# Query stage of a gated cross-attention and expert-attention kernel: VectorE works ahead on the groups of x, transposes are spread between projections, loads are reordered, ScalarE scales the last fifteen tiles

## The chip, the cores and the metric

One core of one Trainium2 chip runs the whole program. The metric is the device time of one execution in microseconds (us), lower is better. The program's engines are TensorE (PE; its weight loads PEld), VectorE (DVE), ScalarE (ACT), GpSimd (POOL) and SyncE (SP, which here only issues transfers). They run their own instruction streams in order and meet at semaphores.

## The reference, cut to what matters

x is 32 batches x 100 tokens x 256, all float32; the context is 32 x 361 x 256.

```
x = x + tanh(g_xattn) * xattn(layernorm(x), ctx)      # 16 heads of 16; q from layernorm(x), k and v from ctx
x = x + tanh(g_ffn) * ffn(layernorm(x))               # 8 heads of 128, attention over 100 tokens,
                                                      # values and outputs through 2 of 8 experts per head
# inside xattn
Q = layernorm(x) @ Wq.T + bq;  K = ctx @ Wk.T + bk;  V = ctx @ Wv.T + bv
O = softmax(mask(Q K^T / 4)) V @ Wo.T + bo
```

## The kernel before

The first half of the program (`stage_attention_in`) runs two parts on every engine, one behind the other in program order: the query stage (`stage_queries`) and the cross-attention (`stage_cross`), with the cross-attention's first steps, `start(0)` to `start(6)`, interleaved into the query stage through `between`. The experts' part follows behind a barrier and isn't touched.

**Query stage.** The 3200 tokens of x are 25 tiles of 128 tokens in `big`, in five groups of five, each group one load (640 KB). Per group, VectorE takes mean and variance of each tile (L246, L249), forms 1/std in small steps with one square root on ScalarE (L136 to L146 and `root`, L277), and scales the five tiles in place (L253). TensorE turns each tile with two transposes into `pt`, which has two banks (L306); ScalarE copies it to `xnt` (L284). Then come the projections: 16 units of 4 matmul records each (128 x 400, L316) into the four banks of `pq`. For each unit ScalarE writes a float16 high part (`hi`, L295) and VectorE the rest (`low`, L259). Groups 0 to 4 own units 0-1, 2-5, 6-7, 8-11 and 12-15. TensorE's unit n waits for `low(n - 4)`.

What orders the work is written out by hand. TensorE: five turns, then the units of the group, `between(n - 4)` behind unit n. VectorE: statistics and scaling of group g + 1, then `low` for the units of group g. ScalarE: five copies, the next group's root, then `hi` for the units.

**First steps of the cross-attention.** `start(0)`: TensorE makes the keys of batch 0 (12 matmuls, L727), ScalarE and VectorE their high and low parts (L653, L548). `start(1)`, `start(2)`: values of batch 0 (12 and 6 matmuls, L744; copies L661). `start(3)`: keys of batch 1. `start(4)`: VectorE spreads a bias (L538, L542). `start(5)`: TensorE's output bias (L821, L822). `start(6)`: VectorE scales it by the tanh of the gate (L610), which ScalarE makes behind the last copies (L291). The keys wait until GpSimd has split weights and two contexts into float16 high and low parts (L224 to L238), and GpSimd waits for all weights and biases (`s_cw`, 96).

**SyncE.** It issues, in order: x0, x1, wq, bq, x2, x3, x4, the gates, wk, wv, wo, three biases, two contexts. Then, per quarter of the queries, `between(g)`, the store of the high part and that of the low part (L208, L211). Behind the last quarter it waits until all four quarters have landed (L470), and only then issues batch 1's eight query loads (L414), its mask and x (L419, L421), and the context of batch 3 (L403), which GpSimd splits (L484, L486) and TensorE turns into keys in batch 1's first steps.

The cross-attention itself takes 16 heads per batch, TensorE's first matmul of each is the score (L755); one reciprocal of the denominators (L574) comes once per batch.

Of the kernel before, what the change touches and what calls it, by code (L numbers as in the profile page):

```python
# [29 lines left out]
P = 128  # L30
# [119 lines left out]
def stage_queries(nc, k, sems, cross, big, x, g_xattn, g_ffn, wq_t, bq, ctx_t, weights, biases, q_parts):  # L150


    with ExitStack() as ctx:
# [7 lines left out]
        std, rstd, half = (m.sbuf(n, [P, NT]) for n in ("q_std", "q_rstd", "q_half"))  # L161
        qhi = m.sbuf("q_hi", [P, DC, T], F16)
# [6 lines left out]
        s_cw, s_cx = held.sem("q_s_cw"), held.sems("q_s_cx", 2)  # L169
        s_zero, s_chi, s_clo = (held.sem(f"q_s_{n}") for n in ("zero", "chi", "clo"))  # L170
        s_g, s_tanh = held.sem("q_s_g"), held.sem("q_s_tanh")
# [5 lines left out]
        SHIFT = 4  # L177
# [6 lines left out]

        def sync(sp, between):
            for i in range(GROUPS):
# [3 lines left out]
                if i == 1:  # L190
                    sp.dma_start(wq[:, :, :], wq_t.rearrange("(c p) e -> p c e", p=P)).then_inc(s_w, 16)
                    sp.dma_start(bqc[:, :], bq).then_inc(s_w, 16)
            for i, g in enumerate((g_xattn, g_ffn)):
                sp.dma_start(k.tanh_g[:, i:i + 1], g.partition_broadcast(P)).then_inc(s_g, 16)
            for i, w in enumerate(weights):
                sp.dma_start(cross.w[:, i, :, :], w.rearrange("(c p) e -> p c e", p=P)).then_inc(s_cw, 16)
            bk, bv, bo = biases
            sp.dma_start(cross.bkc[:, :], bk).then_inc(s_cw, 16)
            sp.dma_start(cross.bvc[:, :], bv).then_inc(s_cw, 16)
            sp.dma_start(cross.bor[:, :], bo.rearrange("(a n) -> a n", a=1)).then_inc(s_cw, 16)  # L200
            for b in range(2):
                sp.dma_start(cross.ctxb[:, b, :, :], ctx_t[b, :, :].rearrange("(c p) s -> p c s", p=P)
                             ).then_inc(s_cx[b], 16)
# [10 lines left out]
        def gpsimd(pool):  # L214
# [8 lines left out]
            pool.wait_ge(s_cw, 96)  # L223
# [17 lines left out]
        def vector(dve, between):  # L241
            def normalize_group(g):
                cut = slice(TILES * g, TILES * (g + 1))
                dve.wait_ge(s_x[g], 16)
                for t in tiles(g):
                    dve.bn_stats(st[:, t, :], xt[:, t, :]).then_inc(s_st, 1)  # L246
                dve.wait_ge(s_st, TILES * (g + 1))
                for t in tiles(g):
                    dve.bn_aggr(mv[:, t, :], st[:, t, :]).then_inc(s_mv, 1)  # L249
                dve.wait_ge(s_mv, TILES * (g + 1))  # L250
                rstd_steps(dve, mv[:, cut, :], std[:, cut], rstd[:, cut], half[:, cut], s_step, s_std, 6 * g)
                for t in tiles(g):
                    dve.tensor_scalar(xt[:, t, :], xt[:, t, :], mv[:, t, 0:1], rstd[:, t:t + 1],  # L253
                                      ALU.subtract, ALU.mult).then_inc(s_xn, 1)
# [10 lines left out]
            normalize_group(0)  # L265
            dve.wait_ge(s_w, 32)
            for g in range(GROUPS):
                if g < GROUPS - 1:
                    normalize_group(g + 1)
                for n in units(g):  # L270
                    low(n)

        def scalar(act, between):
# [4 lines left out]

            root(0)
            act.wait_ge(s_w, 32)  # L280
            for g in range(GROUPS):
                for t in tiles(g):
                    act.wait_ge(s_t, t + 1)
                    act.activation(xnt[:, :, t * P:(t + 1) * P],  # L284
                                   pt[:, t % 2, 0:DC * P].rearrange("p (c n) -> p c n", c=DC),
                                   ACT.Copy).then_inc(s_xnt, 1)
                if g < GROUPS - 1:
                    root(g + 1)
                else:
                    act.wait_ge(s_g, 32)  # L290
                    act.activation(k.tanh_g[:, :], k.tanh_g[:, :], ACT.Tanh).then_inc(s_tanh, 1)  # L291
                for n in units(g):
# [4 lines left out]
                    between(n - SHIFT)  # L297

        def tensor(pe, between):
            pe.wait_ge(s_id, 2)  # L300
            for g in range(GROUPS):
                for t in tiles(g):
                    pe.wait_ge(s_xn, t + 1)
                    at_least(pe, s_xnt, t - 1)
                    for c in range(DC):
                        last = pe.transpose(pt[:, t % 2, c * P:(c + 1) * P],  # L306
                                            xt[:, t, c * P:(c + 1) * P], k.ident[:, :])
                    last.then_inc(s_t, 1)
# [3 lines left out]
                for n in units(g):  # L312
# [7 lines left out]
                    between(n - SHIFT)  # L320

# [8 lines left out]
def stage_cross(nc, k, sems, queries, cross, x, ctx_t, mask, q_parts, k_parts, big, mv, x1):  # L330
# [22 lines left out]
    with ExitStack() as ctx:  # L353
# [46 lines left out]
        def sync_programs(sp):  # L400
# [41 lines left out]
            def start(g):  # L442
                if g == 0:
# [3 lines left out]
                    load_ctx(fixed(2))  # L447
                    stack_keys(fixed(0))
                elif g == 1:
# [6 lines left out]
            def body(b):  # L456
# [79 lines left out]
        def vector_programs(dve):  # L536
            def bias_values():
                dve.memset(ones[:, :], 1.0).then_inc(s_one, 1)  # L538
                dve.wait_ge(s_one, 1)
                dve.wait_ge(queries.s_weights, 96)  # L540
# [178 lines left out]
        def tensor_programs(pe):  # L719
# [86 lines left out]
            def start(n):  # L806
# [9 lines left out]
                elif n == 5:  # L816
                    pe.wait_ge(s_bvb, DC)
                    pe.wait_ge(s_klo, 2 * DC)
                    pe.wait_ge(queries.s_weights, 96)
# [1044 lines left out]
```

## Time and profile before

| | |
|---|---|
| median of 3 runs | 1904.57 us (1901.36 to 1905.35) |
| profiled execution, own time | 1905.3 us, span 1903.5 us |
| mean granted TensorE clock | 0.99 |
| busy over the span | PE 97%, DVE 78%, ACT 59%, POOL 50% |
| query stage (start to first score) | 67.5 us |

The profiled execution takes 1.8 us more than its span, and 0.7 us more than the median. The rows of the trace give start and length in us from the start of the span; a bracket behind a row gives the idle time before it and what ended it. A granted clock of 1.00 is 2.4 GHz, 0.50 is 1.2 GHz.

### The profile page before, as it was taken

What the parts mean: (1) busy time and instruction counts of PE and PEld (TensorE: products, weight loads), DVE (VectorE), ACT (ScalarE), POOL (GpSimd) and SP (SyncE); (2) the same over time, 40 slices, a digit from 0 to 9 for tenths busy, and PEclk for the clock granted to TensorE, in tenths of its full rate; (3) what the DMA queues carried; (4) which work ended last, traced back from release to release, by engine and by line L of the source; (5) the groups of instructions that cost most, each with busy time, mean ns of one, the idle gap of its engine ahead of it and who ended that gap; (6) DMA issues with size and microseconds to landing.
All of it is one profiled execution on the core that took longest, in us unless ns stands there. A gap on an engine that the chain in (4) does not pass through costs nothing. (4 is left out here: it accounts for less than half of the span.)

```text
span 1903.5 us, 57554 instructions
## 1 busy us (share of the span) xinstructions
PE 1850.6 (97%) x13454; PEld 1141.4 (60%) x13454; DVE 1479.6 (78%) x4245; ACT 1129.1 (59%) x3591; POOL 951.6 (50%) x1432
## 2 busy tenths in 40 slices
PE   5899999999979999999999999999999999999998
PEld 3588888888866554444444445545555555555543
DVE  6699999999979833555555566669999999999989
ACT  3689899998976444444444455445555555555543
POOL 4122222222212004666666666656776776767766
PEclk9999999999999999999999999999999999999999
DMA  5544455545513573000000041122222222222201
GB/s 159 139 125 121 121 129 128 125 124 125 132 44 150 232 306 131 14 28 28 28 28 28 15 126 63 56 62 74 75 71 81 71 76 72 76 71 74 75 20 60
DMA packets 161427, 174.20 MB, mean 92 GB/s; under 512 B 49873, under 2 KB 148562, under 8 KB 159314
## 3 DMA queue, kind: packets, MB, share of 16 engines
q1 hardware_dynamic: 159186, 165.05, 29.4%
q0 software_dynamic: 2176, 8.39, 1.3%
q8 instruction: 28, 0.46, 0.1%
q14 instruction: 37, 0.30, 0.1%
HBM read 112.41 MB, written 60.98 MB: 91 GB/s over the span
## 5 line engine op out<-in xcount | busy, mean ns | idle before, releaser
L1502 POOL TENSOR_TENSOR o_side<-o_side,o_tmp 128x256 f32 (+1 forms) x528 | 397.1, 752 | 195.8 <-POOL o_side L1502 72.7
L1271 PE MATMUL e_pv<-e_vw,e_xhi 128*128 (+1 forms) x1600 | 475.9, 379 | 1.2 <-ACT e_out L1194 1.2
L1204 ACT ACTIVATE big<-e_pv,gates 128x128 f32<-128x128 f32 x800 | 227.8, 368 | 280.9 <-PE e_pv L1271 279.4
L1630 ACT ACTIVATE o_tmp<-o_py,gates 128x256 f32<-128x256 f32 x528 | 221.8, 473 | 194.6 <-PE o_py L1702 142.0
L670 ACT ACTIVATE c_ex<-c_sm,c_nmax 100x361 f32<-100x361 f32 x512 | 302.3, 594 | 35.4 <-DVE c_nmax L559 22.5
L1702 PE MATMUL o_py<-o_whi,a_chi 128*128 128x512 f16 x800 | 304.9, 381 | 0.2
L1702 PE MATMUL o_py<-o_wlo,a_chi 128*128 128x512 f16 x800 | 304.4, 381 | 0.0
L1702 PE MATMUL o_py<-o_whi,a_clo 128*128 128x512 f16 x800 | 304.3, 380 | 0.0
L1271 PE MATMUL e_pv<-e_vw,e_xlo 128*128 (+1 forms) x800 | 303.2, 379 | 0.0
L559 DVE CUSTOM_DVE_ANT_0 c_sm<-c_ps,c_mbias 100x361 f32<-100x361 f32 x512 | 270.2, 529 | 35.0 <-PE c_ps L755 28.2
L1137 DVE TENSOR_SCALAR e_acc<-e_pv,gates 128x128 f32<-128x128 f32 x400 | 121.8, 346 | 223.0 <-PE e_pv L1271 222.9
L1562 DVE SCALAR_TENSOR_TENSOR o_main<-o_py,gates,o_main 128x256 f32 (+1 forms) x536 | 256.4, 478 | 36.9 <-issue 20.7
L1271 PEld LDWEIGHTS e_pv<-e_vw,e_xhi 128*128 (+1 forms) x1600 | 156.5, 98 | 186.7 <-issue 1.6
L1562 DVE SCALAR_TENSOR_TENSOR o_side<-o_py,gates,o_side 128x256 f32 (+1 forms) x536 | 254.5, 475 | 0.1
L762 PE MATMUL c_pt<-ident,c_ex 100*121 100x100 f32 x1536 | 237.7, 264 | 1.8 <-DVE c_ext L569 1.1
L1020 POOL TENSOR_TENSOR big<-big 128x256 f32<-128x256 f32 x200 | 144.8, 724 | 170.8 <-ACT big L1204 124.0
L762 PEld LDWEIGHTS c_pt<-ident,c_ex 100*121 100x121 f32 x1536 | 219.4, 185 | 16.8 <-issue 2.3
L755 PE MATMUL c_ps<-c_kst,c_qst 128*100 128x361 f16 x512 | 168.6, 329 | 1.5 <-DVE c_nmax L559 1.2
L569 DVE COPY c_ext<-c_pt 121x300 f32<-121x300 f32 x320 | 148.0, 463 | 10.6 <-PE c_pt L762 8.8
L1613 ACT ACTIVATE a_ex<-a_ps,a_mxs 100x100 f32<-100x100 f32 x256 | 84.5, 342 | 105.4 <-DVE a_mxs L1533 98.9
L1702 PEld LDWEIGHTS o_py<-o_whi,a_clo 128*128 (+1 forms) x800 | 78.4, 98 | 95.5 <-issue 1.4
L1271 PEld LDWEIGHTS e_pv<-e_vw,e_xlo 128*128 (+1 forms) x800 | 78.2, 98 | 94.3
(164 smaller groups left out, 3152.4 us busy)
## 6 DMA issues: line engine op xcount, KB each, us to landing
qk<-e_out SPq DMA_DIRECT2D x16, 1600.0 KB, 5.2
c_kst<-k_parts SPq DMA_DIRECT2D x128, 180.5 KB, 3.4
a_q<-qk SPq DMA_DIRECT2D x64, 200.0 KB, 2.5
a_k<-qk SPq DMA_DIRECT2D x64, 200.0 KB, 2.5
v<-e_out SPq DMA_DIRECT2D x20, 640.0 KB, 3.3
a_v<-v SPq DMA_DIRECT2D x64, 200.0 KB
c_ctx<-in_ctx_t SPq DMA_DIRECT2D x32, 361.0 KB, 3.9
e_wst<-in_v_w POOLq DMA_DIRECT2D x8, 1024.0 KB, 8.2
```

What stands on the lines that cost most here:

```text
L559: dve.tensor_tensor_reduce(out=sm[:, h % 4, :], in0=p_s[0:SQ, h % 2, 0:SK], in1=mbias[:, b.par, :], scale=-0.25 / WS, scalar=BIG, op0=ALU. ...
L569: dve.tensor_copy(ext[:, h % RING, :], p_t[0:KW, h % 2, 0:KC * SQ]).then_inc(s_extd, 1)
L670: act.activation(ex[:, h % 4, 0:SK], sm[:, h % 4, :], ACT.Exp, scale=-1.0, bias=nmax[:, h % 4:h % 4 + 1], accum_out=den[:, b.par, HEAD[h]: ...
L755: pe.matmul(p_s[0:SQ, h % 2, 0:SK], qst[:, b.par, HEAD[h], :], kst[:, b.par, HEAD[h] // 2, :], start=True, stop=True).then_inc(s_s, 1)
L762: last = pe.transpose(p_t[0:KW, h % 2, c * SQ:(c + 1) * SQ], ex[:, h % 4, c * KW:(c + 1) * KW], k.ident[0:SQ, 0:SQ])
L1020: pool.tensor_tensor(tsum[:, hh, :, :], tmp[:, hh, 0:2, :], tmp[:, hh, 2:4, :], ALU.add).then_inc(s_ts, 1)
L1204: act.activation(tmp[:, hh, e, :], p_v[:, hh, 1, e * PD:(e + 1) * PD], ACT.Copy, scale=gate).then_inc(s_av, 1)
L1271: last = pe.matmul(p_v[:, hh, half, :], a[:, c, bass.ds(t * P, P)], vw[:, bass.ds(col + (w * DC + c) * VW, 512)], start=j == 0, stop=j == ...
L1502: pool.tensor_tensor(side[:, x.t, :], side[:, x.t, :], tmp[:, slot(x, r), j, :], ALU.add).then_inc(s_pool, 1)
L1562: dve.scalar_tensor_tensor(out=into[:, x.t, :], in0=p_y[:, q, j, :], scalar=gate, in1=into[:, x.t, :], op0=ALU.mult, op1=ALU.add).then_inc ...
L1630: act.activation(tmp[:, slot(x, r), j, :], p_y[:, q, j, :], ACT.Copy, scale=gate).then_inc(s_av, 1)
L1702: last = pe.matmul(p_y[:, q, :, :].rearrange("p j d -> p (j d)"), a[:, bass.ds(buf * T + x.t * P, P)], b[:, buf, cut], start=j == 0, stop= ...
```

## The change

VectorE runs the statistics of groups 0, 1 and 2 before its first `low`, and those of groups 3 and 4 before `low(4)` and `low(6)`. It scales only the tiles of groups 0 and 1. For groups 2 to 4 it makes a `shift` (minus mean times 1/std) and ScalarE applies it tile by tile (`apply_norm`). On TensorE and ScalarE the tiles of group g + 1 stand between the units of group g (`tiles_beside`). The first steps come one unit earlier (`SHIFT` 3), the tanh comes before group 4's units. SyncE issues x0, wq, bq, x1, wk, wv, bk, context 0, x2, context 1, x3, wo, bv, bo, x4, gates; GpSimd waits for wk, wv and bk alone. The keys of batch 0 are stacked behind the first quarter's stores, and the wait for quarters 1 to 3 moves behind the issues of batch 1.

```diff
-        SHIFT = 4
+        SHIFT = 3
+        BY_ACT = 2
...
+        def tiles_beside(n):
+
+            g = next(g for g in range(GROUPS) if n in units(g))
+            if g == GROUPS - 1:
+                return ()
+            each, i = len(units(g)), n - units(g)[0]
+            return tiles(g + 1)[TILES * i // each:TILES * (i + 1) // each]
...
+            load_x(0)
+            sp.dma_start(wq[:, :, :], wq_t.rearrange("(c p) e -> p c e", p=P)).then_inc(s_w, 16)
+            sp.dma_start(bqc[:, :], bq).then_inc(s_w, 16)
+            load_x(1)
+            for i in range(2):
+                load_weight(i, s_ckv)
+            sp.dma_start(cross.bkc[:, :], bk).then_inc(s_ckv, 16)
+            load_ctx(0)
+            load_x(2)
+            load_ctx(1)
+            load_x(3)
+            load_weight(2, s_cw)
...
+            load_x(4)
...
-            pool.wait_ge(s_cw, 96)
+            pool.wait_ge(s_ckv, 48)
...
+                if g >= BY_ACT:
+                    dve.scalar_tensor_tensor(out=shift[:, cut], in0=mv[:, cut, 0], scalar=-1.0,
+                                             in1=rstd[:, cut], op0=ALU.mult, op1=ALU.mult).then_inc(s_shift, 1)
+                    return
...
-            normalize_group(0)
+            for g in range(3):
+                normalize_group(g)
             dve.wait_ge(s_w, 32)
-            for g in range(GROUPS):
-                if g < GROUPS - 1:
-                    normalize_group(g + 1)
-                for n in units(g):
-                    low(n)
+            for n in range(DC * NC):
+                if n == 4:
+                    normalize_group(3)
+                elif n == 6:
+                    normalize_group(4)
+                low(n)
...
+            def apply_norm(t):
+                if t // TILES < BY_ACT:
+                    return
+                act.wait_ge(s_shift, t // TILES - BY_ACT + 1)
+                act.activation(xt[:, t, :], xt[:, t, :], ACT.Identity, scale=rstd[:, t:t + 1],
+                               bias=shift[:, t:t + 1]).then_inc(s_xna, 1)
...
             root(0)
+            for t in tiles(0):
+                copy_turned(t)
+            root(1)
...
                 for n in units(g):
                     c, w = n % DC, n // DC
                     act.wait_ge(s_q, n + 1)
                     act.activation(qhi[:, c, w * NW:(w + 1) * NW], pq[:, n % 4, 0:NW],
                                    ACT.Identity, bias=bqc[:, c:c + 1]).then_inc(s_hi, 1)
                     between(n - SHIFT)
+                    for t in tiles_beside(n):
+                        apply_norm(t)
+                    for t in tiles_beside(n):
+                        copy_turned(t)
+                if g < GROUPS - 2:
+                    root(g + 2)
+                elif g == GROUPS - 2:
+                    act.wait_ge(s_g, 32)
+                    act.activation(k.tanh_g[:, :], k.tanh_g[:, :], ACT.Tanh).then_inc(s_tanh, 1)
...
                     last.then_inc(s_q, 1)
                     between(n - SHIFT)
+                    for t in tiles_beside(n):
+                        turn(t)
...
-                    stack_keys(fixed(0))
-                elif g == 1:
+                elif g == 1:
+                    stack_keys(fixed(0))
...
+                if isinstance(b.n, int) and b.n == 1:
+                    for g in range(1, 4):
+                        sp.wait_ge(queries.s_stored[g], 32)
...
-                for g in range(4):
-                    sp.wait_ge(queries.s_stored[g], 32)
```

`turn(t)` on TensorE waits for VectorE's scaling (tiles 0 to 9) or ScalarE's (10 to 24), and for the copy of tile t - 2.

## Rows read from the trace of the kernel before

**Rows 1.** Stretches: bounds, length; busy PE, PEld, DVE, ACT, POOL; clock, DMA share, GB/s.

```profile
0.00:67.50 67.50, 44.51 (x163) 25.27 (x163) 39.68 (x128) 24.17 (x55) 23.59 (x24) 0.95 0.51 155
...
81.40:100.35 18.95, 17.07 (x197) 14.23 (x197) 13.95 (x47) 14.13 (x46) 5.99 (x7) 0.91 0.41 100
```

**Rows 2.** The same view, stretches inside the query stage.

```profile
18.00:20.95 2.95, 1.57 (x11) 0.85 (x10) 2.24 (x6) 2.18 (x6) 2.78 (x3) 1.00 0.04 14
...
25.25:30.48 5.23, 0.00 (x0) 0.00 (x0) 4.40 (x6) 0.59 (x1) 4.88 (x5) 1.00 0.00 0
30.48:34.00 3.52, 3.52 (x12) 1.91 (x13) 0.60 (x1) 0.56 (x1) 0.50 (x1) 0.52 0.38 105
...
54.49:58.95 4.46, 4.46 (x9) 2.35 (x9) 0.63 (x1) 0.59 (x1) 0.00 (x0) 0.62 0.58 146
```

**Rows 3.** Timeline (start, length in us): VectorE and ScalarE, groups 0 to 2.

```profile
5.31 1.74 DVE L246 BATCH_NORM_STATS2 q_st<-big 128x6 f32<-128x256 f32 x5 [5.31 <-DMA big<-in_x]
...
14.37 1.71 DVE L253 TENSOR_SCALAR big<-big,q_mv,q_rstd 128x256 f32<-128x256 f32 x5
...
18.08 0.59 ACT L295 ACTIVATE q_hi<-q_pq,q_bq 128x400 f16<-128x400 f32 x1 [1.11 <-PE q_pq L316]
...
18.57 0.65 ACT L284 ACTIVATE q_xnt<-q_pt 128x256 f32<-128x256 f32 x2
...
22.60 0.59 ACT L295 ACTIVATE q_hi<-q_pq,q_bq 128x400 f16<-128x400 f32 x1 [0.61 <-PE q_pq L316]
...
23.34 4.68 DVE L253 TENSOR_SCALAR big<-big,q_mv,q_rstd 128x256 f32<-128x256 f32 x5
```

**Rows 4.** L316 by stretch: length, PE busy (records), clock, DMA share, GB/s.

```profile
13.30:16.01 2.71, 2.67 (x4) 1.00 1.11 330
20.95:22.28 1.33, 1.33 (x4) 1.00 0.00 0
```

**Rows 5.** Timeline of GpSimd: the first of its splits, and one later.

```profile
16.61 0.25 POOL L224 TENSOR_SCALAR c_bk<-c_bk 128x2 f32<-128x2 f32 x1 [9.22 <-DMA c_bo<-in_bo]
...
26.32 1.55 POOL L238 TENSOR_TENSOR c_ctxlo<-c_ctx,c_ctxhi 128x722 f16<-128x722 f32 x1
```

**Rows 6.** L253 alone, one stretch of group 2's five: length, DVE busy, clock, DMA.

```profile
26.40:27.80 1.40, 1.40 (x1) 1.00 0.00 0
```

**Rows 7.** ScalarE's groups by shape: busy us, mean ns, idle before.

```profile
L284 ACT ACTIVATE q_xnt<-q_pt 128x256 f32<-128x256 f32 x25 | 8.7, 382 | 5.8 <-PE q_pt L306 5.8
...
L1630 ACT ACTIVATE o_tmp<-o_py,gates 128x256 f32<-128x256 f32 x528 | 221.8, 473 | 194.6 <-PE o_py L1702 142.0 <-POOL o_side L1502 50.1 <-issue 2.4
...
L1166 ACT ACTIVATE e_shi<-e_sst 128x256 f16<-128x256 f32 x1 | 0.4, 416 | 0.7 <-DMA e_sst<-in_sel 0.7
```

**Rows 8.** Timeline around the output bias, and the tanh's table load.

```profile
52.07 0.17 DVE L538 MEMSET c_ones<- 128x128 f32 x1
...
52.81 1.13 PE L821 MATMUL c_pp<-c_w,c_bvb 128*128 128x256 f32 x4 [1.99 <-DVE c_bvb L542]
...
61.98 1.28 ACT L291 ACT_TABLE_LOAD   x1
```

**Rows 9.** Timeline of SyncE behind the query stage.

```profile
68.98 0.37 SPq L211 DMA_DIRECT2D q_parts<-q_lo  x1
72.14 3.67 SPq L414 DMA_DIRECT2D c_qst<-q_parts  x8
...
76.66 1.26 SPq L403 DMA_DIRECT2D c_ctx<-in_ctx_t  x1
```

**Rows 10.** Timeline: TensorE and VectorE in batches 0 to 2.

```profile
83.60 0.33 PE L727 MATMUL c_pp<-c_ctxhi,c_whi 128*128 128x361 f16 x1 [1.87 <-POOL c_ctxlo L486]
...
87.09 0.25 DVE L574 RECIPROCAL c_rden<-c_den 100x16 f32<-100x16 f32 x1
103.57 0.25 DVE L574 RECIPROCAL c_rden<-c_den 100x16 f32<-100x16 f32 x1
118.86 0.25 DVE L574 RECIPROCAL c_rden<-c_den 100x16 f32<-100x16 f32 x1
```

More of the change, by code:

```diff
@@ L161, in stage_queries @@
         std, rstd, half = (m.sbuf(n, [P, NT]) for n in ("q_std", "q_rstd", "q_half"))
+        shift = m.sbuf("q_shift", [P, NT])
         qhi = m.sbuf("q_hi", [P, DC, T], F16)
@@ L183, in units, with load_x @@
             return range(*(TILES * n * P // NW * DC for n in (g, g + 1)))
+        def tiles_beside(n):
[4 more added lines that the diff above has]
+            return tiles(g + 1)[TILES * i // each:TILES * (i + 1) // each]
         def sync(sp, between):
-            for i in range(GROUPS):
+            bk, bv, bo = biases
+            def load_x(i):
                 sp.dma_start(xt[:, TILES * i:TILES * (i + 1), :],
@@ L189, in sync, with load_weight, load_ctx @@
                              ).then_inc(s_x[i], 16)
-                if i == 1:
-                    sp.dma_start(wq[:, :, :], wq_t.rearrange("(c p) e -> p c e", p=P)).then_inc(s_w, 16)
-                    sp.dma_start(bqc[:, :], bq).then_inc(s_w, 16)
+            def load_weight(i, landed):
+                sp.dma_start(cross.w[:, i, :, :], weights[i].rearrange("(c p) e -> p c e", p=P)
+                             ).then_inc(landed, 16)
+            def load_ctx(b):
+                sp.dma_start(cross.ctxb[:, b, :, :], ctx_t[b, :, :].rearrange("(c p) s -> p c s", p=P)
+                             ).then_inc(s_cx[b], 16)
+            load_x(0)
[10 more added lines that the diff above has]
+            load_weight(2, s_cw)
+            sp.dma_start(cross.bvc[:, :], bv).then_inc(s_cw, 16)
+            sp.dma_start(cross.bor[:, :], bo.rearrange("(a n) -> a n", a=1)).then_inc(s_cw, 16)
+            load_x(4)
             for i, g in enumerate((g_xattn, g_ffn)):
                 sp.dma_start(k.tanh_g[:, i:i + 1], g.partition_broadcast(P)).then_inc(s_g, 16)
[L195 to L203, printed above, removed]
             for g in range(4):
@@ L277, in root, with copy_turned @@
                 act.activation(std[:, cut], mv[:, cut, 1], ACT.Sqrt).then_inc(s_std, 1)
+            def apply_norm(t):
[4 more added lines that the diff above has]
+                               bias=shift[:, t:t + 1]).then_inc(s_xna, 1)
+            def copy_turned(t):
+                act.wait_ge(s_t, t + 1)
+                act.activation(xnt[:, :, t * P:(t + 1) * P],
+                               pt[:, t % 2, 0:DC * P].rearrange("p (c n) -> p c n", c=DC),
+                               ACT.Copy).then_inc(s_xnt, 1)
             root(0)
+            for t in tiles(0):
+                copy_turned(t)
+            root(1)
             act.wait_ge(s_w, 32)
             for g in range(GROUPS):
[L282 to L291, printed above, removed]
                 for n in units(g):
@@ L297, in scalar, with turn @@
                     between(n - SHIFT)
-        def tensor(pe, between):
+                    for t in tiles_beside(n):
[7 more added lines that the diff above has]
+                    act.activation(k.tanh_g[:, :], k.tanh_g[:, :], ACT.Tanh).then_inc(s_tanh, 1)
+        def tensor(pe, between):
+            def turn(t):
+                if t // TILES < BY_ACT:
+                    pe.wait_ge(s_xn, t + 1)
+                else:
+                    pe.wait_ge(s_xna, t - TILES * BY_ACT + 1)
+                at_least(pe, s_xnt, t - 1)
+                for c in range(DC):
+                    last = pe.transpose(pt[:, t % 2, c * P:(c + 1) * P],
+                                        xt[:, t, c * P:(c + 1) * P], k.ident[:, :])
+                last.then_inc(s_t, 1)
             pe.wait_ge(s_id, 2)
+            for t in tiles(0):
+                turn(t)
             for g in range(GROUPS):
[L302 to L308, printed above, removed]
                 if g == 0:
@@ L320, in tensor @@
                     between(n - SHIFT)
+                    for t in tiles_beside(n):
+                        turn(t)
         programs = Programs()
```

7 lines of the change are left out of this document (4 added, 3 removed).

## The prediction

> **What bounds the kernel now.** I read first the table of stretches. The query stage lasts 67.50 us, in which TensorE is busy for 44.51; nothing else is near it (VectorE 39.68, ScalarE 24.17) [rows 1]. The stage ends when TensorE has done its last unit, because the scores of batch 0 follow on the same engine at once. So the ledger to keep is TensorE's: its work in order, and each wait between.
>
> In that ledger a unit, four records of L316, takes 1.33 us at full clock and 2.67 at half [rows 4]. From the start of unit 2 at 20.95 to 67.50 there are 46.55 us. The work at full clock is 14 units (18.7), 24 keys matmuls at 0.15 (half the 0.30 that 12 take of the 3.52 us at half clock [rows 2]: 3.65), 18 value matmuls at 0.11 (1.95), the output bias (1.68, from 52.81 to the next unit at 54.49 [rows 2, 8]) and 15 turned tiles at 0.27 (4.1): 30.1. The other 16.4 are waits and half clock. The largest wait is 5.23 us for GpSimd's splits [rows 2], which run from 16.61 to the keys at 30.48, 13.9 us, and begin only when the last bias has landed [rows 2, 5]. Then 1.99 us for the bias chain on VectorE [rows 8]. After both the granted clock fell to 1.2 GHz for about 3.4 us: the four records and the keys behind them took double [rows 2]. At full clock 3.52 us of keys would have been 1.8, so a fall costs 1.7. Groups whose five turns stand together wait 1.4 us each (1.57 busy of 2.95, and no fall behind it [rows 2]).
>
> Behind the stage the timeline shows one more wait that this change touches: TensorE idles 1.87 us in batch 1 for the split of batch 3's context, which SyncE issued at 76.66, behind query loads that began at 72.14 although the last store was issued at 68.98 [rows 9, 10]. The clock falls again in that batch: 0.91 over 18.95 us is 3.4 us at half clock [rows 1].
>
> **The change part by part.** I go along TensorE, whose instructions stay in order.
>
> *Loads.* bk now has 2.1 MB in front of it. The first 0.66 MB landed at 5.31 [rows 3], and 0.33 MB a microsecond from there [rows 4] puts bk near 9.8 instead of before 16.6. GpSimd's 13.9 us then end near 23.7, before unit 3 is through, so the 5.23 us wait for the keys goes. x2 lands near 12.5, x3 near 15.5, x4 near 18; VectorE wants them at 16, 29 and 40, so the reordering costs nothing there.
>
> *VectorE ahead, and beside GpSimd.* In group 1 five scalings take 1.71 us; in group 2 they take 4.68, and GpSimd is busy throughout [rows 3]. From 26.40 to 27.80 VectorE has a single scaling in hand, where one takes 0.34 in group 1, beside GpSimd's one instruction from 26.32 to 27.87 [rows 5, 6]. So I let one scaling end per GpSimd instruction. With GpSimd from 9.8 on, group 1's scaling, from 14.37, no longer ends at 16.08 but near 19.9; if GpSimd's first long instruction also catches the last tile of group 0, which starts near 10.4, everything on VectorE comes 1.3 later and the end is 21.4. Beside that row stands the Trainium skill, "SBUF — State Buffer", section "SBUF: two separate sides": whichever of the two engines starts first holds the port pair they share for its whole instruction, and the other blocks. The trace agrees with it in that stretch. By the mean of group 2 (0.94 a tile) the end would be 19.1, unit 3 would start 0.8 earlier, and so would everything below.
>
> Group 2's statistics follow (2.5 us to the root and 1.5 for the small steps and the shift: about the time that group 2's take now), so the shift is there at 24.0 to 25.2. Unit 2 runs from 21 to 22.4; tile 10 must be scaled and turned before unit 3. Unit 3 starts at 25.0 to 26.1; without any collision it would be 23.3. I take 25.5.
>
> *The turn between two units.* This is the core. ScalarE does `hi(n)`, then scales tile t, and TensorE can turn t only then, and only then take unit n + 1. A `hi` starts 1.65 us after its unit (20.95 to 22.60 [rows 3, 4]), of which 1.33 is the unit. The next ScalarE instruction starts 0.49 later (18.08 to 18.57 [rows 3]). The scaling on ScalarE isn't in the trace. Its nearest rows are 0.382 (the copy of 256 columns), 0.416 (256 columns from SBUF) and 0.473 (256 columns with a scale per row) [rows 7]; I take 0.42, since it reads SBUF. With 0.1 to TensorE and 0.27 for the turn, the time from unit to unit is 1.65 + 0.49 + 0.42 + 0.1 + 0.27 = 2.93, of which 1.33 are idle. Where keys or values stand behind the unit, ScalarE's copies of them come ahead of the scaling, and the idle is about the same. Two or three tiles add the waits for `pt`'s two banks. From 25.5:
>
> unit 4 at 30.2 (keys 1.83 between), unit 5 at 34.3 (values 1.3), unit 6 at 38.65 (values 0.65, tiles 13 and 14), unit 7 at 43.7 (keys 1.83, tiles 15 and 16), unit 8 at 48.4 (three tiles, 2.45 of its 4.7 idle). Now the bias: VectorE is held in group 4's steps until ScalarE's root at 48.3, then needs 1.3 for the steps, 2.3 for `low(6)`, two key parts and `low(7)` at 0.57, and 0.74 from the ones to TensorE [rows 8]: the bias starts at 52.7, TensorE idle for 3.0 where it is 1.99 now. Unit 9 at 54.7, 10 at 57.65, 11 at 60.6, 12 at 64.4 (two tiles), and four units end at 69.8. The tanh and its table load (1.5 us, 1.28 of it the load [rows 8]) lie beside units 12 and 13; `low(10)`, queued behind it on VectorE, ends at 67.0, when unit 14 wants its bank. So the first score stands at 69.8 with a full clock: 2.3 later than now.
>
> *The clock.* Both waits of 2 us or more had a fall behind them, the one of 1.87 too; half-busy stretches did not [rows 1, 2]. The new stage has 2 to 2.4 us idle ahead of unit 3's turn, 2.45 spread ahead of unit 8, 3.0 ahead of the bias. I count two falls that cost: the first at the full 1.7 (unit 3 and the keys), the second at 1.2 (a third of it lies in idle time; a fall at unit 8 itself would be covered by the wait for the bias). First score at 72.7, which is 5.2 later.
>
> *SyncE.* Behind the last store the loads of batch 1 and context 3 no longer wait for the landing: 2.75 earlier against the first score (69.4 for 72.14). GpSimd's split then ends 1 us before TensorE asks, so the 1.87 goes, and probably the fall behind it (1.7): at most 3.6. The reciprocals bound it from the other side: 16.48 us apart in batches 0 to 1, 15.29 in 1 to 2 [rows 10], so 1.2 was lost behind the first of them and 1.87 ahead of it. I take 3.0 (1.9 to 3.6). The stores of quarters and the keys' stacking for batch 1 are issued 15 us or more ahead of use, as now. Nothing later is touched.
>
> **Sum.** +2.3 + 2.9 - 3.0 = +2.2 on the profiled 1905.3, and the same on the median of 1904.57: 1906.8.
>
> **The rivals.** A measurement of this kernel tells about 0.2% (3.8 us) from no change.
>
> Slower, by the clock: the spread turns leave TensorE 55% busy from unit 2 on, and each further fall costs up to 1.7. For: three waits above 2 us, and the cross-attention's 1.87 had its own fall. Against: 1.57 busy of 2.95 had none [rows 2]. From the third costly fall the sum is +3.9, with four +5.6, with no relief of the clock in batch 1 another +1.1: 1908.5 to 1911.
>
> Slower, by the port: one scaling per GpSimd instruction, group 0's last tile caught too. Unit 3 at 26.1 and the steps slowed, +0.6 to +1.5: 1907.4 to 1908.3. The page named above would have it so; the row in group 2 is one stretch of five.
>
> Faster: the idle ahead of a turn is shorter than I make it. At 0.9 instead of 1.33 in ten places it is 4.3 less, -2.1: 1902.5; with no costly fall besides, -5: 1899.6. It decides from 0.75 a place, or 0.95 with one fall fewer. For it speaks that ScalarE has time; against, that all four steps of the 1.33 are in rows and in series.
>
> The change doesn't do what it says: GpSimd's splits aren't earlier because bk lands late. The keys would wait up to 5 us, but GpSimd would then leave group 1's scaling alone (unit 3 at 23.3): +4 to +5.
>
> **How the numbers follow.** Forecast with its own range 1904 to 1908.4: 0.48. Clock 0.20, port 0.10, late bk 0.05, faster 0.17. Range to leave out 2 in 10: from 1901, a measured half of the faster case, to 1912. Slower by over 0.2%: most of the clock's, half of the port's, the late bk and some of the forecast's, 0.35. Faster: 0.15. Same: 0.50.
>
> **What would show it.** GpSimd's L224 near 10 and its last split near 24. Group 1's L253 at 3.5 us or more. TensorE's idle ahead of each of L306's turns at 1.2 to 1.4, ended by ScalarE. The bias's L821 behind a wait of about 3. First L755 at 69.8 plus falls. No wait ahead of L727 in batch 1, and reciprocals 15.3 apart from the first. Wrong if the turns' idle is below 0.9, if the clock stays up throughout, or if the new stage's first score comes before 68.

## The result, and the profile after

The changed kernel takes 1910.88 us (median of 11 runs, 1903.5 to 1913.36), the kernel before 1902.93 us on the same chip (11 runs, 1900.61 to 1905.35). The ratio is 1.0039, 95% interval 1.0031 to 1.0047: slower by about 7.4 us. The forecast was 1906.8 with a range of 1901 to 1912. The time lies inside the range, 4.1 us above the forecast, and on the side of "slower by over 0.2%", which had 0.35. It is where the rival "slower, by the clock" was placed (1908.5 to 1911). But 1906.8 stood on the 1904.57 of three runs, and eleven runs of before have 1902.93: 1.6 us of the nearness come from the base. Taken as a change, +2.2 was forecast and +7.4 to +8.0 came.

The profiled execution takes 1911.07 us, its span is 1909.3. Line numbers moved: statistics L271, VectorE's scaling L282, shift L278, turns L353, units L368, `hi` L332, ScalarE's scaling L314, copy L319, keys L782, score L810, bias L876, reciprocal L629, GpSimd's splits L249 to L263, context load L457, its split L539 and L541.

Stretches of the changed kernel, same columns as [rows 1]: to the first score, a stretch behind unit 3, one behind unit 9, and batch 1.

```profile
0.00:74.30 74.30, 47.07 (x162) 24.46 (x163) 36.10 (x116) 32.38 (x70) 23.39 (x24) 0.95 0.46 141
25.92:29.92 4.00, 4.00 (x13) 1.87 (x12) 1.30 (x3) 0.98 (x2) 0.00 (x0) 0.57 0.21 77
57.46:61.78 4.32, 3.15 (x7) 1.29 (x7) 0.63 (x1) 1.46 (x3) 0.00 (x0) 0.65 0.40 113
88.00:106.00 18.00, 16.44 (x193) 13.78 (x193) 13.50 (x48) 13.71 (x45) 5.66 (x7) 0.91 0.42 104
```

The stage is 6.8 us longer than in [rows 1]. TensorE is busy for only 2.6 us more; the rest is idle. Its waits in the stage, grouped by who ended them (us in total, times, longest):

```profile
PE q_pt L353 <- ACT big L314: 10.8, 9, 2.0
PE q_pt L353 <- DVE big L282: 9.9, 2, 9.6
PE c_pp L876 <- DVE c_bvb L597: 2.5, 1, 2.5
PE q_pq L368 <- ACT q_xnt L319: 2.5, 5, 0.6
```

The first row is the change: nine turns for which ScalarE's scaling was late. The 9.6 in the second is the start of the program. The wait for GpSimd's splits [rows 2] is gone. Now GpSimd and VectorE in the changed kernel's timeline, the answer to [rows 3, 5]:

```profile
10.36 0.47 POOL L249 TENSOR_SCALAR c_bk<-c_bk 128x2 f32<-128x2 f32 x1 [2.97 <-DMA c_bk<-in_bk]
...
22.52 1.56 POOL L263 TENSOR_TENSOR c_ctxlo<-c_ctx,c_ctxhi 128x722 f16<-128x722 f32 x1
```

```profile
13.81 1.16 DVE L142 TENSOR_TENSOR q_half<-q_half,q_mv 128x5 f32<-128x5 f32 x1
...
15.79 3.64 DVE L282 TENSOR_SCALAR big<-big,q_mv,q_rstd 128x256 f32<-128x256 f32 x5
...
22.57 1.52 DVE L142 TENSOR_TENSOR q_half<-q_half,q_mv 128x5 f32<-128x5 f32 x1
```

The splits run from 10.36 to 24.08, as forecast (9.8 to 23.7), and group 1's scaling, 1.71 us before, takes 3.64 beside them. The price of two single small steps, 0.17 us elsewhere and 1.16 and 1.52 here, was not in the forecast.

TensorE's timeline, with one whole period of the new order, units 10 to 11, and ScalarE's part of such a period behind unit 4:

```profile
25.65 0.44 PE L353 MATMUL q_pt<-ident,big 128*128 128x128 f32 x2 [1.96 <-ACT big L314]
...
55.30 1.13 PE L876 MATMUL c_pp<-c_w,c_bvb 128*128 128x256 f32 x4 [2.46 <-DVE c_bvb L597]
...
61.78 1.51 PE L368 MATMUL q_pq<-q_xnt,q_wq 128*128 128x400 f32 x4
64.47 0.44 PE L353 MATMUL q_pt<-ident,big 128*128 128x128 f32 x2 [1.17 <-ACT big L314]
64.74 1.51 PE L368 MATMUL q_pq<-q_xnt,q_wq 128*128 128x400 f32 x4
...
74.30 0.32 PE L810 MATMUL c_ps<-c_kst,c_qst 128*100 128x361 f16 x1
```

```profile
33.93 0.59 ACT L332 ACTIVATE q_hi<-q_pq,q_bq 128x400 f16<-128x400 f32 x1 [0.96 <-PE q_pq L368]
...
35.52 0.59 ACT L314 ACTIVATE big<-big,q_shift,q_rstd 128x256 f32<-128x256 f32 x1
36.63 0.38 ACT L319 ACTIVATE q_xnt<-q_pt 128x256 f32<-128x256 f32 x1 [0.53 <-PE q_pt L353]
```

From unit 10 to unit 11 it is 2.96 us (forecast 2.93), 1.17 of them idle (forecast 1.33). The bias waits 2.46 (forecast 3.0). Behind the stage SyncE's batch 1 loads begin right behind the last store, 1.9 us behind the first score, where it had been 4.6 [rows 9]; but in this execution the context lands late and TensorE still waits. SyncE, TensorE and the reciprocals, to be read against [rows 9, 10]:

```profile
75.79 0.37 SPq L236 DMA_DIRECT2D q_parts<-q_lo  x1
76.21 4.33 SPq L468 DMA_DIRECT2D c_qst<-q_parts  x8
...
81.38 0.39 SPq L457 DMA_DIRECT2D c_ctx<-in_ctx_t  x1
```

```profile
89.95 0.33 PE L782 MATMUL c_pp<-c_ctxhi,c_whi 128*128 128x361 f16 x1 [1.40 <-POOL c_ctxlo L541]
```

```profile
93.70 0.25 DVE L629 RECIPROCAL c_rden<-c_den 100x16 f32<-100x16 f32 x1
109.86 0.25 DVE L629 RECIPROCAL c_rden<-c_den 100x16 f32<-100x16 f32 x1
125.51 0.25 DVE L629 RECIPROCAL c_rden<-c_den 100x16 f32<-100x16 f32 x1
```

### The profile page after: what moved, and what is told of

The parts are those of the page before. It is cut to its first block and busy times, and to the rows that moved or that the text cites. A ratio compares the mean times of both kernels' runs of the same rounds, so it can differ in the third digit from the quotient of the medians.

```text
span 1909.3 us, 57556 instructions
## 1 busy us (share of the span) xinstructions
PE 1852.5 (97%) x13454; PEld 1140.2 (60%) x13454; DVE 1475.1 (77%) x4233; ACT 1139.7 (60%) x3606; POOL 952.1 (50%) x1432
## 5 line engine op out<-in xcount | busy, mean ns | idle before, releaser
L810 PE MATMUL c_ps<-c_kst,c_qst 128*100 128x361 f16 x512 | 168.6, 329 | 1.5 <-DVE c_nmax L614 1.2
L624 DVE COPY c_ext<-c_pt 121x300 f32<-121x300 f32 x320 | 147.8, 462 | 11.8 <-PE c_pt L817 9.9
```

The lines of the kernel that those rows point to most:

```text
L624: dve.tensor_copy(ext[:, h % RING, :], p_t[0:KW, h % 2, 0:KC * SQ]).then_inc(s_extd, 1)
L810: pe.matmul(p_s[0:SQ, h % 2, 0:SK], qst[:, b.par, HEAD[h], :], kst[:, b.par, HEAD[h] // 2, :], start=True, stop=True).then_inc(s_s, 1)
```

## The experiments

A fall here is a stretch in which the granted clock is down at 1.2 GHz. Four theories were to be told apart: the series (ScalarE's scaling stands between a unit and the next, and that idle time is the loss), the clock (it is held down by the half-busy stretches), the late landing (behind the stage the relief is missing because the context comes late), and the port (VectorE's scaling waits beside GpSimd). Each kernel's edit is against the changed kernel unless said otherwise. The figures of all, the trace's ones each from one execution:

| kernel | median us (runs) | ratio to before, 95% | first score | 1st, 2nd reciprocal | half clock in the stage |
|---|---|---|---|---|---|
| before | 1902.93 (11) | | 67.50 | 87.09, 103.57 | 6.8 |
| changed | 1910.88 (11) | 1.0039, 1.0031 to 1.0047 | 74.30 | 93.70, 109.86 | 6.8 |
| e1 | 1899.05 (11) | 0.9982, 0.9973 to 0.9992 | 66.17 | 83.34, 98.69 | 10.2 |
| e2 | 1898.99 (11) | 0.9982, 0.9973 to 0.9991 | 64.11 | 81.42, 96.77 | 6.8 |
| e3 | 1897.65 (7) | 0.9964, 0.9952 to 0.9976 | 62.43 | 83.65, 100.01 | 6.8 |
| e4 | 1911.43 (5) | 1.0045, 1.0031 to 1.0058 | 77.62 | 94.80, 110.14 | 17.1 |
| e5 | 1910.46 (6) | 1.0035, 1.0023 to 1.0047 | 75.61 | 92.78, 108.13 | 13.7 |
| e6 | 1900.95 (12) | 0.9992, 0.9983 to 1.0000 | 68.43 | 85.61, 100.95 | 10.2 |
| e7 | 1894.86 (6) | 0.9966, 0.9954 to 0.9978 | 59.98 | 77.15, 92.49 | 0 |
| e8 | 1895.23 (5) | 0.9963, 0.9951 to 0.9976 | 60.19 | 77.37, 92.71 | 3.4 |
| e9 | 1907.62 (9) | 1.0024, 1.0014 to 1.0034 | 74.92 | 92.09, 107.44 | 6.8 |
| e10 | 1892.48 (5) | 0.9944, 0.9931 to 0.9957 | 58.31 | 75.48, 90.83 | 0 |
| e11 | 1912.39 (6) | 1.0053, 1.0035 to 1.0071 | 78.98 | 96.16, 111.50 | 17.1 |
| e12 | 1899.52 (10) | 0.9983, 0.9974 to 0.9993 | 62.91 | 80.08, 95.42 | 3.4 |

Each ratio is to runs of before on the same chip, which had medians of 1902.27 to 1903.54. The last column, in us, is the sum of (1 - granted clock) x 2 x length over windows of 0.5 us.

**e1: ScalarE scales ahead of waiting for the unit.**

```diff
                     c, w = n % DC, n // DC
+                    for t in tiles_beside(n):
+                        apply_norm(t)
                     act.wait_ge(s_q, n + 1)
...
-                    for t in tiles_beside(n):
-                        apply_norm(t)
```

> The changed kernel with one edit: ScalarE scales the tiles beside unit n before it waits for unit n, not behind its high part. Theory A (the series unit, high part, scaling, turn is what costs, about 1.3 us idle at ten places): the idle ahead of the turns of tiles 10 to 24 goes except for the wait for the first of them, the time from unit to unit with one tile falls from 2.96 to about 1.6, the first score comes 9 to 12 us earlier (62 to 65 for 74.3), and the time is 7 to 11 us below the changed kernel, so 1 to 4 below the one before. Theory B (the clock's falls are what costs, the spread turns only feed them): the turns' idle shrinks but the falls stay, first score near 71, 3 us gained.

1899.05 us, faster than before too, and less than the changed kernel by 11.8 us on the medians, 10.8 on the ratios. In its timeline the four last units start at 60.69 where they started at 68.83, and only two turns still wait for a scaling (2.6 us in all, 1.98 of it ahead of unit 3):

```profile
59.83 0.27 PE L353 MATMUL q_pt<-ident,big 128*128 128x128 f32 x1
60.69 5.64 PE L368 MATMUL q_pq<-q_xnt,q_wq 128*128 128x400 f32 x16 [0.59 <-ACT q_xnt L319]
66.17 0.32 PE L810 MATMUL c_ps<-c_kst,c_qst 128*100 128x361 f16 x1
```

It does the same work on the same engines in another order on one of them, and its stage held more half clock in the trace (10.2 us for 6.8), not less; over its eleven runs the mean granted clock of the program is 0.9919, over the 17 of the changed kernel 0.9916. So the gain isn't the clock's, and the series is the main loss.

**e2: VectorE scales all tiles.** The turns stay between the units.

```diff
-        BY_ACT = 2
+        BY_ACT = 5
```

> The changed kernel with BY_ACT = 5: VectorE scales all 25 tiles, ScalarE none; everything else stays. Theory A: the turns no longer stand behind ScalarE's high parts, so most of the 1.3 us places go; against that VectorE takes 15 more scalings (0.34 each, 5.1 us in all) of which five (1.7) lie ahead of the output bias. First score near 66, 6 to 9 us below the changed kernel, a little worse than scaling ahead on ScalarE. Theory B (VectorE needs the relief that ScalarE gives): first score no earlier than 74, time not below the changed kernel.

1898.99 us: behind unit 3 no turn waits for its scaling, so spread turns cost little when the tile is ready. What it loses is at the bias, where VectorE is now later still; its timeline:

```profile
47.75 2.07 PE L876 MATMUL c_pp<-c_w,c_bvb 128*128 128x256 f32 x4 [4.36 <-DVE c_bvb L597]
```

**e3: the kernel before, with the new order of loads alone** (and GpSimd waiting for wk, wv and bk).

```diff
-            pool.wait_ge(s_cw, 96)
+            pool.wait_ge(s_ckv, 48)
...
+            load_x(0)
...
+            for i in range(2):
+                load_weight(i, s_ckv)
+            sp.dma_start(cross.bkc[:, :], bk).then_inc(s_ckv, 16)
+            load_ctx(0)
+            load_x(2)
```

> The kernel before with only the new order of loads and GpSimd's earlier start (wait for wk, wv, bk alone). Theory A: the 5.2 us wait for the keys goes and the clock's fall behind it (1.7), while the scaling of group 1 beside GpSimd takes 3 us more, 1 of them on TensorE's way: first score near 62, 4 to 6 us below the kernel before. Theory B (the collision with GpSimd eats what the earlier splits give): first score at 66 or later, within 2 us of the kernel before.

1897.65 us, 4.6 less than the 1902.27 of before beside it, 6.9 by the ratio. The 5.23 us wait for the splits is gone, the first score stands 5.1 earlier.

**e4: the context of batch 3 is loaded ahead of batch 1's queries.**

```diff
+                if is_first(b):
+                    load_ctx(later(b, 3))
...
-                if later(b, 3):
+                if later(b, 3) and not is_first(b):
```

> The changed kernel with the load of batch 3's context issued ahead of batch 1's eight query loads instead of behind them. Theory C (the relief of 3.0 us failed because the context stood in the transfer queue behind the stores and query loads): the split of context 3 ends before TensorE asks, no wait ahead of the keys in batch 1 and no fall of the clock, first two reciprocals 15.3 to 15.5 us apart instead of 16.16, 2 to 3 us below the changed kernel. Theory D (nothing to be had there, batch 0 and 1 are bound by VectorE and ScalarE): the wait goes but the time stays within 1 us.

The trace shows the relief whole: 17.18 us from first score to first reciprocal (19.40 in the changed kernel), 15.34 to the next (16.16). The time is that of the changed kernel. What the change's trace lacked is there in the trace of e5, the same kernel unedited, and in nine further ones with SyncE's moved wait and the context behind the query loads: landing after 3.3 to 4.5 us, first two reciprocals 15.34 or 15.35 apart. So the late landing explains one execution and not the median.

**e5: the changed kernel once more, unedited.**

> The changed kernel once more, unchanged, for a second trace. Theory A with the clock's part: the stage's order is the same, so every wait between units repeats within 0.2 us, while the number and length of the clock's falls differs, and the first score moves with them between 72 and 78. If instead the falls are fixed by the order, the first score stands at 74.3 again. Theory C (the context stands in the queue): its landing takes 5.9 us again and TensorE waits 1.4 us in batch 1. Theory E (that landing was that run's own): it lands in about 4.4 us and the two first reciprocals are 15.4 apart.

Same time, 1910.46, and a trace that differs in three places: the wait ahead of unit 3, the clock behind the bias, and the landing of the context. TensorE, the reciprocals and GpSimd:

```profile
25.11 0.44 PE L353 MATMUL q_pt<-ident,big 128*128 128x128 f32 x2 [2.54 <-ACT big L314]
25.39 1.51 PE L368 MATMUL q_pq<-q_xnt,q_wq 128*128 128x400 f32 x4
...
60.16 2.87 PE L368 MATMUL q_pq<-q_xnt,q_wq 128*128 128x400 f32 x4
64.21 0.69 PE L353 MATMUL q_pt<-ident,big 128*128 128x128 f32 x2 [1.17 <-ACT big L314]
64.69 2.87 PE L368 MATMUL q_pq<-q_xnt,q_wq 128*128 128x400 f32 x4
...
75.61 0.32 PE L810 MATMUL c_ps<-c_kst,c_qst 128*100 128x361 f16 x1
```

```profile
92.78 0.25 DVE L629 RECIPROCAL c_rden<-c_den 100x16 f32<-100x16 f32 x1
108.13 0.25 DVE L629 RECIPROCAL c_rden<-c_den 100x16 f32<-100x16 f32 x1
```

```profile
87.08 0.79 POOL L539 CAST c_ctxhi<-c_ctx 128x722 f16<-128x722 f32 x1 [2.70 <-PE c_pp L799]
```

Here 2.54 us of idle ahead of unit 3 had no fall behind it (unit 3 takes 1.51). Nor had 3.40 in e4, while 3.57 in e8 had one of 3.4 us; the two rows:

```profile
25.20 0.44 PE L353 MATMUL q_pt<-ident,big 128*128 128x128 f32 x2 [3.40 <-ACT big L314]
```

```profile
25.27 0.44 PE L382 MATMUL q_pt<-ident,big 128*128 128x128 f32 x2 [3.57 <-ACT big L343]
```

But in e5, from behind the bias on, the clock is at 1.2 GHz for 13.7 us, over units 9, 10 and 11, and unit 10 to 11 is 4.53 us for 2.96. A stretch of that, and the same batch 1 lengths as the relief asked for: 17.17 from the first score and 15.35, the context landing 3.5 us after its issue, where it was 5.9 in the first trace.

```profile
53.10:68.70 15.60, 12.12 (x24) 5.51 (x24) 1.11 (x2) 4.41 (x10) 0.00 (x0) 0.56 0.34 97
```

**e6: the kernel before, SyncE's wait for quarters 1 to 3 moved behind batch 1's issues.**

```diff
+                if isinstance(b.n, int) and b.n == 1:
+                    for g in range(1, 4):
+                        sp.wait_ge(queries.s_stored[g], 32)
 
             def rest():
-                for g in range(4):
-                    sp.wait_ge(queries.s_stored[g], 32)
```

> The kernel before with only SyncE's wait for the quarters moved behind batch 1's issues. Theory E (the relief behind the stage is real, 3 us): the query stage is unchanged, TensorE doesn't wait in batch 1, no fall of the clock there, first score to first reciprocal 17.3 for 19.6, 2 to 3 us below the kernel before. Theory C (the transfer queue hides it): TensorE still waits 1.4 us, within 1 us of the kernel before.

1900.95 us, 2.4 less than its before (1903.31), 1.5 by the ratio, whose interval reaches 1.0000. From first score to second reciprocal it is 32.52 us, 36.07 before: the forecast's relief, shown by itself in the trace. **e7 has both edits, e3's and e6's.**

> The kernel before with the new order of loads, GpSimd's earlier start and SyncE's moved wait; VectorE, ScalarE and TensorE keep the old order. Theory A: the two parts add, 4.6 from the loads and 3 from the wait, about 1895, and it beats the version that scales ahead on ScalarE (1899), since the turns in one block cost 1.4 us per group and no more. Rival: the spread turns with scaling ahead are worth something by themselves, then this stays at 1898 or above.

1894.86 us, 8.4 below the 1903.31, 6.5 by the ratio. The two parts alone gave 4.6 and 2.4 by the medians, 6.9 and 1.5 by the ratios, so that they add is likely but not shown to better than 2 us. Its trace has no fall in the stage although the bias waits 1.99 us, while e3's, the same stage on TensorE, falls for 6.8 us behind a wait of 2.00. The bias rows of e7 and e3, and a stretch behind each:

```profile
46.96 1.13 PE L836 MATMUL c_pp<-c_w,c_bvb 128*128 128x256 f32 x4 [1.99 <-DVE c_bvb L557]
```

```profile
46.23 1.13 PE L835 MATMUL c_pp<-c_w,c_bvb 128*128 128x256 f32 x4 [2.00 <-DVE c_bvb L556]
```

```profile
47.00:51.00 4.00, 4.00 (x13) 2.36 (x14) 0.53 (x2) 0.59 (x1) 0.00 (x0) 1.00 0.32 92
```

```profile
47.30:54.30 7.00, 7.00 (x14) 3.61 (x14) 0.63 (x1) 0.81 (x2) 0.00 (x0) 0.51 0.42 106
```

**e8: e1, and VectorE's small steps of groups 3 and 4 stand apart from their statistics**, behind `low(5)` and `low(7)`.

```diff
                 if n == 4:
-                    normalize_group(3)
+                    measure_group(3)
                 elif n == 6:
-                    normalize_group(4)
+                    scale_group(3)
+                    measure_group(4)
+                elif n == 8:
+                    scale_group(4)
```

> The version that scales ahead on ScalarE, with VectorE's small steps of groups 3 and 4 moved behind the low parts of units 5 and 7, so that the output bias no longer waits for group 4's root. Theory A: TensorE's wait ahead of the output bias falls from 2.46 to under 1 and the clock's fall behind it goes or shortens, first score near 63 for 66.2, 2 to 4 us below that version, about 1896. Rival (only the place of the wait moves, to group 4's first turn): within 1 us of it.

1895.23 us, 3.8 less than e1; the bias no longer waits. That is the level of e7 (1894.86), which has the old order and still the bias's wait; the old order without that wait, e10 below, is lower. So nothing speaks for the spread turns by themselves.

**e9: the idle time ahead of the turns is filled.** Two matmuls more behind each of units 2 to 11, into the bank of the next unit, which overwrites them; nothing reads their result.

```diff
+                    if 2 <= n < 12:
+                        at_least(pe, s_lo, n - 2)
+                        for _ in range(2):
+                            pe.matmul(pq[:, (n + 1) % 4, 0:256], wq[:, 0, 0:P], xnt[:, 0, 0:256],
+                                      start=True, stop=True)
```

> The changed kernel with two extra matmuls (128x256 float32, their result is overwritten by the next unit) on TensorE ahead of the turns behind units 2 to 11, so that it works through most of the 1.17 us that it waits for ScalarE's scaling. The order and the waits of the other engines stay. Theory F (half of the loss is the clock: once down, the half-busy stretch of units 9 to 11 keeps it at 1.2 GHz for 13.7 us in two of three traces): the clock comes back within 3.4 us of each fall, first score at 70 to 73, 2 to 4 us below the changed kernel in spite of the extra work. Theory A alone (only the waits in series count): the extra work is at best hidden, first score at 74 or later, time the same or above.

1907.62 us, 3 less than the changed kernel, with more work; the clock theory expected 2 to 4. Its other signs didn't come in this one trace: the first score stands at 74.92 and not at 70 to 73, and the fall behind the bias lasts 6.8 us and not 3.4. The period stays 2.96 us, the idle ahead of a turn is 0.31; its timeline:

```profile
62.40 1.51 PE L368 MATMUL q_pq<-q_xnt,q_wq 128*128 128x400 f32 x4
63.75 1.03 PE L376 MATMUL q_pq<-q_xnt,q_wq 128*128 128x256 f32 x4
65.08 0.44 PE L353 MATMUL q_pt<-ident,big 128*128 128x128 f32 x2 [0.31 <-ACT big L314]
65.36 1.51 PE L368 MATMUL q_pq<-q_xnt,q_wq 128*128 128x400 f32 x4
```

Over its nine runs the mean granted clock of the whole program is 0.9939, over the 17 of the changed kernel 0.9916. That speaks for the clock theory, with about 3 us, but doesn't prove it: the intervals of the two kernels' ratios overlap.

**e10: e7, with group 4's small steps and scaling on VectorE behind `low(9)` and the bias.**

```diff
-                if g < GROUPS - 1:
+                if g < GROUPS - 2:
                     normalize_group(g + 1)
+                elif g == GROUPS - 2:
+                    measure_group(g + 1)
                 for n in units(g):
+                    if n == 10:
+                        scale_group(4)
```

> The kernel before with the new loads and the moved wait, and on VectorE the small steps and the scaling of group 4 behind low(9) and the bias values instead of ahead of low(8). Expected: TensorE's wait of 1.99 ahead of the output bias goes, the turns of group 4 wait up to 1 us more for their scaling, first score 1 to 2 us ahead of 59.98, about 1893.5, the lowest of all versions. Rival: the wait moves to the turns of group 4 in full, then it equals the version without this edit (1894.9).

1892.48 us, the best of all, 0.56% below before (0.43 to 0.69). The bias waits 0.67 us; the stage is 58.31 long:

```profile
0.00:58.31 58.31, 41.77 (x162) 24.06 (x163) 39.49 (x128) 24.16 (x55) 23.65 (x24) 1.00 0.59 180
```

**e11: GpSimd's splits wait until group 1 is scaled.**

```diff
             pool.wait_ge(s_ckv, 48)
+            pool.wait_ge(s_xn, 10)
```

> The changed kernel with GpSimd's splits held until VectorE has scaled its ten tiles. Port theory: the five scalings of group 1 take 1.71 us again for 3.44 and 3.64, small steps 0.17 each, unit 3 starts near 23 for 25.4 to 25.9. Against that the splits end near 30 and the keys of batch 0 wait 5 to 6 us for them as in the kernel before, so that unit 4 comes about 1 us later than in the changed kernel: the collision costs less than the early splits give, time 0 to 3 us above the changed kernel. Rival (it's not GpSimd that slows the scalings): they take over 3 us in this run too.

1912.39 us. VectorE is free of GpSimd, and the keys are late. VectorE, then TensorE:

```profile
13.89 0.17 DVE L142 TENSOR_TENSOR q_half<-q_half,q_mv 128x5 f32<-128x5 f32 x1
...
14.50 1.70 DVE L283 TENSOR_SCALAR big<-big,q_mv,q_rstd 128x256 f32<-128x256 f32 x5
```

```profile
30.11 0.48 PE L783 MATMUL c_pp<-c_ctxhi,c_whi 128*128 128x361 f16 x1 [4.65 <-POOLq L547]
```

So the port's price is real (3.64 us beside GpSimd, 1.70 without). Unit 3 starts at 23.95, 1.4 to 2.0 us earlier than in the changed kernel's two traces, but unit 4 at 35.53, 3.2 to 5.4 later (1 was expected), with a fall of 10.2 us around it. On the time, 1912.39 for 1910.88, the intervals of the ratios overlap: holding the splits gains nothing.

**e12: e2 with fifteen small ScalarE instructions more.** In the changed kernel's two traces, e1, e4, e8, e9 and e11, the time from the second to the last reciprocal is 458.0 to 458.1 us; in before, e2, e3, e6, e7 and e10 it is 456.6. The first are the kernels in which ScalarE scales tiles.

```diff
+                if 2 * TILES <= t:
+                    act.activation(shift[:, t:t + 1], std[:, 0:1], ACT.Copy)
                 if t // TILES < BY_ACT:
                     return
```

> The kernel of e2 (VectorE scales all 25 tiles) with fifteen more ScalarE instructions, each a copy of one column into a tile that nothing reads, at the places where the changed kernel scales tiles 10 to 24. What it is for: in the seven traces in which ScalarE scales tiles, the time from the second to the thirty-second reciprocal is 458.0 to 458.1 us, with batch 1 to 2 at 15.65 and every second batch 0.10 us longer; in the six traces without it (e2 among them) it is 456.6, with batch 1 to 2 at 15.28. Theory A: what counts is how many instructions stand in ScalarE's stream ahead of the cross-attention, not what they do. Then this kernel shows 458.0 and 15.65, and its median stands 1.5 us above that of e2 (1900.5 for 1899.0). Theory B: it comes from something else that the kernels with ScalarE's scaling share (VectorE's twelve instructions fewer, or x written by ScalarE). Then 456.6 and 15.28 stay, and the median is that of e2, plus 0.2 to 1 us for the fifteen small copies in the query stage (the first score within 1.5 us of e2's 64.1).

456.57 us, and 15.29 for batch 1 to 2. The count of ScalarE's instructions isn't the cause. The median is 1899.52, 0.5 above e2's, within what the intervals allow.

## Why the prediction was right, and where it was off

Right: the side of TensorE that it kept a ledger of. Here is its sum against the two traces of the changed kernel, each less the trace of before. A fall's cost is the gap between two units less the same gap at full clock: 4.32 less 2.96 behind unit 9; 6.46 from unit 3 to 4 (25.92 to 32.38) less the 4.77 of e5's trace (25.39 to 30.16); and so on.

| part | forecast | first trace | e5's trace |
|---|---|---|---|
| first score, cost of falls taken out | +2.3 (69.8) | +3.6 (71.1) | +3.1 (70.6) |
| falls in the stage | +2.9 | +3.2 | +5.0 |
| first score to second reciprocal | -3.0 | -0.5 | -3.6 |
| second to last reciprocal | 0 | +1.5 | +1.5 |
| behind the last reciprocal | 0 | -1.9 | +0.2 |
| sum | +2.2 | +5.8 | +6.2 |

The last part differs between executions, 1341.2 to 1343.9 us over the fourteen traces, in no order of kernels. The profiled run of before, at 1905.3, was the slowest of its 11, which is why the traces differ by less than the medians (7.4 to 8.0).

*Loads and splits*: right, and worth 4.6 to 6.9 us by themselves (e3). *Beside GpSimd*: right; unit 3 was forecast at 25.5 and started at 25.92 and 25.39. The Trainium skill ("SBUF — State Buffer", "SBUF: two separate sides") says that, for the VectorE operations that use the ports the two share, whichever engine starts first holds them and the other one blocks. e11 agrees that they collide, and here it was VectorE that waited: 1.70 us for 3.64, while GpSimd's own L251 and L254 take 1.49 to 1.58 in the changed kernel and 1.49 to 1.51 in e11.

*The turn between two units*: 2.93 forecast, 2.96 measured, but of other parts. ScalarE's scaling takes 0.59 us where 0.42 was taken, and several in a row follow each other at 0.49, so gaps with two and three tiles came out longer; the `hi` starts 0.1 earlier. Together with unit 3 these make the 0.8 to 1.3 us by which the first score is late at full clock. e1 proves the reading: the same scaling taken out of the series gives 11 to 12 us back. The 2.67 us that the forecast took for a unit at half clock are unit 0's [rows 4], and stand beside a granted clock of 1.00, as 2.6 to 2.7 us of unit 0 do in all eight traces read there; why is open. A unit at half clock is e5's 2.87 for 1.51. No term of the sum changes by it.

*SyncE*: right; 3.55 us in e5, 3.55 in e6. The first trace, with the context landing after 5.9 us, was the only one of twelve with the moved wait that lacked it.

*The step that failed is the clock.* The forecast put two falls of 3.4 us in the stage, cost 2.9, and none in batch 1; it took the length of a fall from [rows 2], where both were 3.4. In the half-busy stretch behind the bias a fall can last: 13.7 us in e4 and e5. Even the old order has 6.8 us there in e3 and e6. The forecast held that unlikely by one row, 1.57 busy of 2.95 without a fall, which is one stretch of 3 us between busy ones. Over all executions the mean clock is 0.9916 in 17 of the changed kernel and 0.9921 in 68 of before: 0.0005 x 2 x 1909 = 1.9 us more at half clock, up to 0.9 us of time. By the scatter of the runs this 0.9 is uncertain by 1.2 either way. Forecast was a gain there: three falls of before at 1.7 each, against two at 2.9 together, is -2.2, or -1.6 with what the relief of 3.0 took of the third. That is 2.5 to 3.1 us missed, with the same uncertainty.

*The second is "nothing later is touched".* 1.5 us are lost between the second and the last reciprocal: 0.36 in batch 1 to 2 (15.65 us for 15.29), then 0.10 in every second batch. It comes with ScalarE's scaling and not with the spread turns (e2) nor the number of instructions (e12). That ScalarE writes x, or that VectorE has fewer instructions, is left, untested. Its cause stays open.

The three together, 2.5 to 3.1, 1.5 and 0.8 to 1.3, are 4.8 to 5.9 us; from +2.2 that gives +7.0 to +8.1, and 7.4 to 8.0 was measured. That they meet so well is in part luck, since the clock's share alone is uncertain by 1.2. So the number was near for half a reason: ledger and signs held, the base came down by 1.6, and the clock rival's mechanism, priced there at 0.20, ran alongside.

Open: what makes a fall come and how long it lasts; the landing after 5.9 us; the 1.5 us.

## What to carry to other kernels

Before an elementwise step is given to an engine with time to spare, look at what stands in front of it in that engine's order: behind an instruction that waits for TensorE it is in series with TensorE, and moving it ahead of that wait (e1) was worth 11 to 12 us, where the step is 0.59 and nine turns of TensorE waited for it. Try the parts of a change alone: its loads and its moved wait were worth 6.5 to 8.4 us together, and the new order of the engines took 13 to 16 away. A stretch that is half idle can have a price beyond its idle time (13.7 us at half clock in e4 and e5), and one trace doesn't tell its size: read the mean granted clock of every run.

## What the runs showed of the hardware

- The same wait has a fall behind it in one execution and none in another: ahead of unit 3, 1.96 us (first trace) and 3.57 (e8) with one, 2.54 (e5) and 3.40 (e4) without; 2.00 at the bias with one (e3), 1.99 without (e7). Falls lasted 3.4, 6.8, 10.2 and 13.7 us, and those of e4 and e11 ahead of the last units (3.4 each) have no wait over 1.2 us in the 10 us before them.
- Time follows the granted clock from run to run. Of the changed kernel, three runs at 0.990 have a mean of 1912.1 us, five at 0.992 1909.3, the one at 0.994 is 1903.5; of before, 19 runs at 0.991 have 1904.0, five at 0.994 1900.7.
- ScalarE's activation of 128 x 256 float32 from SBUF to SBUF, with scale and bias per row, takes 0.589 us and 0.49 in a row; the copy of as many columns out of PSUM takes 0.383.
- Beside GpSimd VectorE's smallest instructions wait as well: 1.16 and 1.52 us for a step on 128 x 5 that takes 0.17. Its statistics of a group don't: 1.72 to 1.73 us beside GpSimd's splits (changed kernel) and 1.72 without them (before).
